# Inverse RMS sent over DRAM, scalings late in their slot, first slots reordered, five weight pieces split later

## What is computed

```python
x = layernorm(x) * w + b ; x = (x + tanh(cond @ lin)) * w + b
def _rmsnorm(x):
    return x * jax.lax.rsqrt(jnp.mean(x * x, axis=-1, keepdims=True) + EPS)
def _ada_rmsnorm(x, t, gamma_w, beta_w):
    gamma = (t @ gamma_w.T)[:, None, :]
    beta = (t @ beta_w.T)[:, None, :]
    return gamma * _rmsnorm(x) + beta
x = x + a_alpha * _attention(_ada_rmsnorm(x, t, attn_gamma_w, attn_beta_w), W_q, W_k, W_v, W_o)
return x + f_alpha * _swiglu(_ada_rmsnorm(x, t, ffn_gamma_w, ffn_beta_w), gate_w, hidden_w, out_w, out_b)
```

## Time and profile before

| | us |
|---|---|
| runs of the kernel, median of 3 | 1015.37 (1011.99 to 1016.5) |
| profiled execution, device time | 1012.19 |
| its span | 1010.4 |
| TensorE busy in it | 964.5 (95%) |
| VectorE busy | 691.4 (68%) |
| ScalarE busy | 625.8 (62%) |
| GpSimd busy | 565.9 (56%) |

### The profile page before, as it was taken

One profiled execution on the slowest core, in us unless ns is written; L12 is line 12 of the kernel. 1 busy time (PEld: TensorE's weight loads), 2 busy tenths in 40 slices (PEclk: granted clock), 3 DMA queues, 4 the chain that ended last, 5 costly groups with the idle time before them and its releaser, 6 DMA issues.

```text
span 1010.4 us, 28503 instructions
## 1 busy us (share of the span) xinstructions
PE 964.5 (95%) x11164; PEld 900.0 (89%) x11164; DVE 691.4 (68%) x1347; ACT 625.8 (62%) x1775; POOL 565.9 (56%) x532
## 2 busy tenths in 40 slices
PE   5576999999999999999999999999999999999997
PEld 4455999999999999999999999999999999998897
DVE  6677676676777667677766767776777676666564
ACT  4556666667666666666666666666666666665432
POOL 4476646566564656656465665656565574443321
PEclk9899999999999999999999999999999999999999
DMA  6100001010100101010010101000000000000000
GB/s 209 43 22 22 2 12 33 12 33 2 33 13 12 33 12 33 2 33 12 12 33 13 32 2 34 12 13 32 13 25 9 13 12 13 12 13 12 12 12 21
DMA packets 20916, 23.36 MB, mean 23 GB/s; under 512 B 1200, under 2 KB 20272, under 8 KB 20784
## 3 DMA queue, kind: packets, MB, share of 16 engines
q1 hardware_dynamic: 20784, 21.54, 6.5%
HBM read 13.15 MB, written 8.39 MB: 21 GB/s over the span
## 4 chain that ended last, share of the span: by engine, by line
PE 86%; DVE 5%; issue 4%; ACT 3%; POOL 1%; DMA 0%; POOLq 0%; SPq 0%; ACTq 0%; DVEq 0%
PE psum L283 17%; PE psum L285 16%; PE psum L284 16%; PE psum L475 6%; PE psum L474 6%; PE psum L473 5%; PE psum L409 5%; PE psum L398 4%; PE psum L420 4%; PE psum L332 2%; PE psum L313 2%; ACT probs L826 2%; PE psum L321 1%; DVE least L585 1%; PE psum L469 1%
## 5 line engine op out<-in xcount | busy, mean ns | idle before, releaser
L283 PE MATMUL psum<-xf_hi,ffn_hi 128*128 128x256 f32 x1024 | 287.5, 281 | 4.2 <-DVE normed_f L633 1.6
L285 PE MATMUL psum<-xf_hi,ffn_lo 128*128 128x256 f32 x1024 | 285.9, 279 | 0.0
L284 PE MATMUL psum<-xf_lo,ffn_hi 128*128 128x256 f32 x1024 | 285.8, 279 | 0.0
L826 ACT ACTIVATE probs<-psum,least 128x64 f32<-128x64 f32 x976 | 213.0, 331 | 53.5 <-DVE least L585 30.0
L656 DVE SCALAR_TENSOR_TENSOR late<-tanh,psum 128x512 f32<-128x512 f32 x128 | 88.0, 687 | 188.7 <-ACT tanh L849 188.7
L283 PEld LDWEIGHTS psum<-xf_hi,ffn_hi 128*128 128x128 f32 x1024 | 192.2, 188 | 5.7 <-issue 4.4
L855 ACT ACTIVATE prod_hi<-late 128x512 fp32r<-128x512 f32 x128 | 80.7, 631 | 187.9 <-DVE late L664 129.0
L285 PEld LDWEIGHTS psum<-xf_hi,ffn_lo 128*128 128x128 f32 x1024 | 192.4, 188 | 0.0
L284 PEld LDWEIGHTS psum<-xf_lo,ffn_hi 128*128 128x128 f32 x1024 | 191.8, 187 | 0.0
L1006 POOL TENSOR_TENSOR probs<-probs,inv_sum 128x512 f32<-128x512 f32 x128 | 139.7, 1091 | 76.7 <-DVE inv_sum L606 76.2
L475 PE MATMUL psum<-prod_hi,ffn_lo 128*128 128x256 f32 x512 | 143.6, 281 | 0.0
(11 more groups left out here) (103 smaller groups left out, 2215.6 us busy)
## 6 DMA issues: line engine op xcount, KB each, us to landing
out_t_dram<-x_res SPq DMA_DIRECT2D x32, 256.0 KB, 2.1
xin<-x_dram SPq DMA_DIRECT2D x15, 512.0 KB, 3.9
w_raw<-attn_w_dram SPq DMA_DIRECT2D x1, 1024.0 KB, 7.0
x_res<-gate_w_dram SPq DMA_DIRECT2D x1, 1024.0 KB, 9.7
late<-hidden_w_dram SPq DMA_DIRECT2D x1, 1024.0 KB, 11.7
x_res<-out_w_dram SPq DMA_DIRECT2D x1, 1024.0 KB, 5.6
xin<-x_dram SPq DMA_DIRECT2D x2, 256.0 KB, 2.9
k_heads<-mod_w_dram SPq DMA_DIRECT2D x1, 320.0 KB, 4.6
```

What stands on the lines that cost most here:

```text
L283: pe.matmul(out, stat_hi, mov_hi, start=first, stop=False)
L284: pe.matmul(out, stat_hi, mov_lo, start=False, stop=False)
L285: return pe.matmul(out, stat_lo, mov_hi, start=False, stop=last)
L826: op = act.activation(probs[g % 2][:, h * SEQ:(h + 1) * SEQ], scores[:, h // 2, h % 2], ACT.Exp, bias=least[g % 2][:, h:h + 1], scale=-1.0)
```

## The change

It has five parts.

1. From group 0 on, SyncE sends the inverses to DRAM and reads them back broadcast over all partitions into a new tile `inverse`. TensorE's transposes for this fall away (two stay for each of the groups -2 and -1), and so do its waits for the scalings. The squares are turned in another order of tokens (`token_cols`: every second column), so that a partition writes two neighbouring numbers.
2. `scale_a` and `scale_f` read `inverse` in SBUF instead of the norm bank in PSUM. They stand at the end of VectorE's slot j = 2, `ffn_split_lo` at the end of slot j = 3. ScalarE's `split_hi_a` and `split_hi_f` stand behind the exponentials of slot j = 3 instead of in front of them, GpSimd's betas in slot j = 3.
3. The first slots: group -1's spreading moves from slot -2 to 0, `keys(1)`, `queries(1)`, `values(1)` from slots 0, 1, 2 to 1, 2, 3.
4. The output weights load into the freed `w_raw`. The pieces of weights are split in another order, five of them in slots 9 to 14. VectorE's half comes one slot behind ScalarE's. The first gates and downs wait for the pieces they need only.
5. The last part's FFN result is gated and added on VectorE and stored in two halves.

```diff
-SPLITS = {-4: (0, 1), -3: (2,), -2: (3,), 0: (4,), 1: (5,), 2: (6,), 3: (7,), 4: (8,), 5: (9,), 6: (10,), 7: (11,)}
-OUT_W_AT = -1
+SPLITS = {-4: (0, 2), -3: (4,), -2: (6,), 1: (5,), 3: (7,), 6: (8,), 9: (1,), 11: (3,), 12: (9,), 13: (10,), 14: (11,)}
+OUT_W_AT = -3
...
+            def spread_inverses(grp):
+                which = slice(0 if is_part(grp + 2) else 1, 2 if is_part(grp - 2) else 1)
+                sp.wait_ge(inv_made, grp + 3)
+                sp.dma_start(inv_dram[grp % 2].rearrange("(w p i) -> p w i", w=2, i=2)[:, which],
+                             mean_sq[:].rearrange("p (w i) -> p w i", i=2)[:, which]).then_inc(inv_stored, 16)
+                if grp >= 2:
+                    sp.wait_ge(scaled_a, min(grp + 1, NPART))
+                if grp >= 4:
+                    sp.wait_ge(scaled_f, grp - 3)
+                sp.wait_ge(inv_stored, 16 * (grp + 1))
+                cols = slice(which.start * PART, which.stop * PART)
+                sp.dma_start(inverse[grp % 2][:, cols], inv_dram[grp % 2:grp % 2 + 1, cols].partition_broadcast(P)
+                             ).then_inc(spread_loaded, 16)
...
-                if norm_step(s) == 2 and is_group(grp) and s >= -4:
-                    spread_inverses(grp)
...
             def scale_f(m):
-                dve.wait_ge(inv_spread, m + 5)
                 dve.wait_ge(gamma_f, m + 1)
-                scale_by_rms(normed_f, PART).then_inc(scaled_f, 1)
+                dve.wait_ge(spread_loaded, 16 * (m + 3))
+                scale_by_rms(normed_f, inverse[m % 2][:, PART:2 * PART]).then_inc(scaled_f, 1)
...
-                if norm_step(s) == 2 and is_part(grp + 2):
-                    scale_a(grp + 2)
...
-                if j == 2 and is_part(grp - 2):
-                    scale_f(grp - 2)
...
-                if j == 3 and is_part(grp - 2):
-                    ffn_split_lo(grp - 2)
...
                 if is_step(f):
                     product(f)
+                if j == 2 and s >= 0 and is_part(grp + 2):
+                    scale_a(grp + 2)
+                if j == 2 and is_part(grp - 2):
+                    scale_f(grp - 2)
+                if j == 3 and is_part(grp - 2):
+                    ffn_split_lo(grp - 2)
...
-                for c in SPLITS.get(s, ()):
+                for c in SPLITS.get(s if s < 0 else s - 1, ()) if s != 0 else ():
                     split_ffn_weights(c)
...
-                if j == 3 and is_part(grp + 2) and s != -1:
-                    split_hi_a(grp + 2)
-                if j == 3 and is_part(grp - 2):
-                    split_hi_f(grp - 2)
...
                 if is_seq(s):
                     exponentials(s)
+                if j == 3 and s >= 0 and is_part(grp + 2):
+                    split_hi_a(grp + 2)
+                if j == 3 and is_part(grp - 2):
+                    split_hi_f(grp - 2)
                 if is_step(f):
                     half_tanh(f)
```

More of the change, by code:

```diff
@@ L135, in conditioned_block @@
         prod_lo = [sb(f"prod_lo{i}", [P, BLK], F32R) for i in range(2)]
+        inv_dram = nc.dram_tensor("inv_dram", [2, 2 * PART], F32).ap()
+        inverse = [sb(f"inverse{i}", [P, 2 * PART]) for i in range(2)]
         gated_f = late[:, 0:KT * PART].rearrange("p (k c) -> p k c", k=KT)
         prod, act_gate = late[:, 2 * BLK:3 * BLK], late[:, 3 * BLK:4 * BLK]
-        ffn_raw = [x_res[:, 3:5].rearrange("p b k c -> p (b k c)"), late[:]]
+        ffn_raw = [x_res[:, 3:5].rearrange("p b k c -> p (b k c)"), late[:], w_raw[:]]
         mod_stage = k_heads[0:COND].rearrange("p a b c d -> p (a b c d)")
@@ L329, in spread_inverses @@
                 pe.wait_ge(inv_made, grp + 3)
-                cols = norm_cols(grp, 1)
-                for i in range(cols.start, cols.stop):
+                for i in range(2):
                     mm = pe.transpose(norm_bank[:, i * P:(i + 1) * P], mean_sq[:, i:i + 1].broadcast_to([P, P]),
@@ L491, in _ @@
                     score(s)
+                if s == 0:
+                    spread_inverses(-1)
+                    values(0)
+                    norm_bank_read(2, -1)
+                if s == 1:
+                    keys(1)
                 norm_bank_free(s)
@@ L507, in _ @@
                     modulation(F_GAMMA, 3)
-                if s == 0:
-                    values(0)
-                if j == 0 and is_part(grp + 1):
+                if j == 0 and is_part(grp + 1) and grp != 0:
                     keys(grp + 1)
-                if j == 1 and is_part(grp + 1):
+                if j == 1 and is_part(grp + 1) and grp != 0:
                     queries(grp + 1)
@@ L515, in _ @@
                     turn_squares(grp)
-                if j == 2 and 1 <= grp + 1 < NPART:
+                if j == 2 and 2 <= grp + 1 < NPART:
                     values(grp + 1)
+                if s == 2:
+                    queries(1)
+                if s == 3:
+                    values(1)
                 if j == 3 and is_part(grp - 1):
@@ L671, in product_lo, with gate_part @@
                                   ).then_inc(prod_lo_made, 1)
+            def gate_part(m, mt):
+                return dve.scalar_tensor_tensor(out=by_seq(gated_f[:, mt]),
+                                                in0=by_seq(y_bank[:, mt * PART:(mt + 1) * PART]),
+                                                scalar=vecs[:, OUT_B, mt:mt + 1], in1=kt_mod(F_ALPHA, mt, m),
+                                                op0=ALU.add, op1=ALU.mult)
             def gate_ffn(m):
@@ L717, in _ @@
                         centre(s)
+                if s == FIRST_SLOT + 2:
+                    scale_a(0)
+                if s == 0:
+                    scale_a(1)
                 if j == 0 and is_part(grp + 2):
@@ L1026, in _ @@
                 if s == 0:
+                    apply_beta_a(1)
                     split_lo_a(1)
```

120 lines of the change are left out of this document (79 added, 41 removed).

## The result

| | before | after |
|---|---|---|
| median of the runs, us | 1013.9 (1011.99 to 1016.5, 4 runs) | 1117.27 (1116.61 to 1117.92, 4 runs) |
| profiled execution, us | 1012.19 | 1116.61 |
| its span, us | 1010.4 | 1114.7 |

The changed kernel takes 1.101 times as long, with an interval of 1.099 to 1.104. The direction was predicted, the size was not: 1117 lies 31 us above the upper end of the range.

What follows compares the result with a forecast made beforehand. TensorE was taken as the bound, by only 0.5 to 0.9 us per group over the VectorE-ScalarE chain. 1012.2 + 64.8 (groups) + 1 (late splits) - 10 (opening) - 2 (end) = 1066 us, range 1030 to 1086.

Steps and rivals of the forecast that it cites:

- TensorE loses the bound to the loop: Steady groups: the VectorE-ScalarE chain from one `find_least` to the next, with GpSimd collisions, outlasts TensorE's 29.15 us; chance 0.60.
- That the tanh would be hidden: Rival, behind slot j = 3: slack swallows the later tanh, TensorE stays the bound, total 990 us; chance 0.08.
- the engines would settle into phases without meeting: Rival, steady groups: VectorE and GpSimd miss each other, +1.13 us per group, total 1032 us; chance 0.22.
- The growth per group: Full groups 3 to 29: each grows by 2.4 us through the longer chain and collisions, 27 x 2.4 = +64.8 us.
- the choice of 2.4 over 3.09: Odd groups, `product_lo` behind `scale_f`: VectorE likelier goes first (mean +2.21, taken as +2.4); GpSimd first would give +3.09.
- The even step from 3 to 0: Even groups, slot j = 3's minima to the next: later tanh +0.84 and collisions +1.06, giving 8.98 us.
- The step from 1 to 2: Minima of slot j = 1 to those of j = 2: the bare VectorE-ScalarE chain, 6.41 us.
- The opening: First slots, up to slot 12: moved `keys(1)` and fewer, later splits save 10 us, between 5 and 15.
- costed at nothing: the way over DRAM: Inverses to the scalings: two transfers need 5.8 us, the scaling comes 11.2 us later, so no cost.
- one of the prediction's own signs of being wrong: VectorE's scalings: the prediction is wrong if one waits for the load of the inverses.
- Late splits: Slots 12 to 15: four weight pieces split there add two- or three-tenths of a us each, +1 us.
- The end: Last groups, without attention: they keep 0.2 to 0.39 us of TensorE's gain each, last addition and store overlap, -2 us.

Runs made afterwards that it cites:

- parts 3 to 5 alone: Kernel before, given only the new first slots, weight splits and last part; TensorE still spreads the inverses and norm steps keep their old places: 1009.02 us, ratio 0.9945.
- the better order: Changed kernel with scalings behind slot j = 3's minima, high halves behind its tanh, residual sum ahead of `xn_lo`, `merge_stats` a slot later: 1022.86 us, ratio 1.009.
- the earlier splits: Late weight pieces split in earlier slots, in the changed kernel (1116.53 us, ratio 1.099) and in the kernel with only parts 3 to 5 (1011.06 us, 0.9953).

## Why the prediction was off

The direction and the mechanism held. The size failed in the terms of the sum. The range also stopped at 1086, below the 1090 that the sum's own worse end gave.

- **TensorE loses the bound to the loop: right.** TensorE busy 181 of 200 us (forecast 185), waits of `turn_probs` for `activate`, the group at 32.95 (forecast 31 to 32.8, just outside). The high halves delay the tanh by 1.04: 625.70 to 628.34 is 2.64 (forecast 2.6). `scale_a` is held to 1.15 (forecast 1.1). The even step from 2 to 3, 7.87 + 1.83 = 9.70, measured 9.62. That the tanh would be hidden, and that the engines would settle into phases without meeting, are both refuted.
- **The growth per group, 27 x 2.4 = +64.8 forecast, 27 x 3.40 = 91.8 measured: the step that failed first.** It is the choice of 2.4 over 3.09, by the sentence "an instruction right behind another on its engine is the likelier to go ahead". In the odd group `product_lo` stands directly behind `scale_f` (656.40). GpSimd's beta, released by `scale_a`, shows from 656.56, waiting while `scale_f` runs. It gets in first, runs to 657.99, and `product_lo` ends at 658.53, 0.54 later, having taken 1.53. The same happened all 15 times that `product_lo` was recorded right behind `scale_f` (1.5 to 1.6 us each). So the odd step from 2 to 3 is 9.62 and not 8.78. The same at `xf_lo` and `product_lo` of the odd j = 3 (664.51, 665.72, with `normalise_probs` at 665.21 between): 8.71 and not 7.75. Both ends of this choice were worked out, and 3.09 was the other end. With it the term would have been 83 us, 19 of the 27 us missing.
- The even step from 3 to 0 was forecast at 8.98 and measured at 9.51: `mean` of `merge_stats`, 128x4, took 0.71 at 632.92, beside GpSimd's `square_sum_f` from 632.88 to 633.61. The forecast counted only big instructions as able to meet.
- The step from 1 to 2 was forecast at the bare loop, 6.41, and measured at 6.61 in even and odd groups, some 5 us over 27 groups. The minima start 0.77 behind `product_lo` (614.60 and 615.37) where the sum had 0.61. What holds them was not looked into.
- **The opening, -10 forecast, +8.8 measured.** The step "costed at nothing: the way over DRAM" was right for full slots (no wait for the load after slot 10) and was carried over to slots of 4 to 6 us without being worked out there. The way takes 8.1 us: inverses ready at 611.35, store issued at 611.38, load issued at 615.45, landing 4.0 later. I had bounded it at 5.8 from a plain load of 2.9. The load was issued 1.2 us after the store had landed, and it takes longer than that plain one. A scaling waiting for the load was one of the prediction's own signs of being wrong, and it showed here, in slots 2, 6 and 10. Even without it the gain was over-rated: parts 3 to 5 alone bring 3.2 us up to slot 12. The step from slot 0 to 1 did fall as forecast, from 9.34 to 4.67, but the slots from 1 to 12 took 57.4 us instead of 56.0.
- **Late splits, +1 forecast, 3.2 measured beyond the group's growth.** Slots 12 to 15 grew by 6.6, of which 3.4 is any group's. The splits themselves cost 2.6, since slots 14 and 15 lose that much without them. Most of the rest is that this group took 28.73 before, 0.4 less than other odd groups (29.11).
- **The end, -2 forecast, +0.5 measured.** Parts 3 to 5 alone gave 1.0 of the 2. With parts 1 and 2 the same stretch took 1.5 more, and no experiment looked at why.

The four differences, 27.0 + 18.8 + 2.2 + 2.5, make the 50.5 us between 1066 and the profiled 1116.6.

What stays open: moved alone, the scalings (one instruction later, still in the loop) are worth 0.48 us per group and the high halves 0.57, and `xf_lo` makes the group 0.99 longer. The last two are mixed with falls of TensorE's clock. The scalings alone behind the minima in every group, and `xf_lo` out of the loop of the better order, were not tried. Why the clock falls in some groups and not in others is open.

## What to carry to other kernels

When the engine that limits has less than a microsecond of slack to the next chain, add up that chain instruction by instruction before moving work "to the end of a slot": the end of one slot is the front of the next one's chain. Work that hides well stands behind the instruction that another engine is waiting for, not in front of it. A transfer that is hidden in the steady part has to be checked again in the shortest slots. And where two waiting engines could go first, take the worse order into the forecast unless a row shows the better one. Before a difference of two totals is put down to an edit, compare the granted clock slot by slot: here it hid part of the gain of the earlier splits and made a nearly free move look like a loss of 27 us.

## What the runs showed of the hardware

- A waiting GpSimd instruction went ahead of the next VectorE instruction, even when that followed its predecessor at once. Two VectorE instructions in a row with GpSimd waiting came out as 0.68 and 1.53 us, 15 of 15 times in the changed kernel. With each side waiting in turn, beta shows 1.43 us instead of 1.04.
- Not only large instructions are held. The 128x4 `mean` of `merge_stats` took 0.71 us in the mean of 11 beside a GpSimd sum, against 0.17 in the kernel before.
- TensorE's granted clock fell to half in short stretches whose place depends on the order of work on other engines. In the changed kernel TensorE idled 1.7 us ahead of most slots j = 0, and it fell at the start of 6 of 26 groups. With only `xf_lo` moved TensorE idled 3.0 us there, and it fell in 24 of 26. The step from 1 to 2 behind it was longer by 0.7 to 1.1 us in that kernel and not at all in the changed one.
- A store of 2 KB, 8 bytes at a time, to DRAM takes 2.9 us to land, and reading it back broadcast over 128 partitions (256 KB) takes 4.0, where a plain load of 256 KB in the kernel before took 2.9. With the issues between them the round trip is 8.1 us.
